# Graph attention and linear attention on one core: all pairs' k projected ahead of all pairs' q

## The chip, the cores and the metric

The kernel runs on one core of a Trainium2 chip. TensorE multiplies matrices, VectorE and ScalarE work on elements, GpSimd (POOL) scatters, and SyncE (SP) issues most of the DMA transfers. Each engine takes its instructions in the order in which they are written, and waits on semaphores that the others raise. The metric is the time of one execution in device microseconds; lower is better.

## The reference, cut to what matters

`x` has 1250 rows of 768. The layer adds to it a graph network (three attention layers over 21250 edges, 4 heads of 192 each), a linear attention of 12 heads of 64 (256 features), and then a mixture of 8 experts. The change touches the linear attention's projections and, beside them, the first steps of the graph attention.

```python
def softmax_kernel(data, proj, is_query):
    data_dash = einsum('bhnd,md->bhnm', d ** -0.25 * data, proj)
    diag = sum(data * data, -1) * 0.5 * (d ** -0.25) ** 2
    m = max(data_dash, -1) if is_query else max(data_dash, (-3, -2, -1))
    return ratio * (exp(data_dash - diag - m) + EPS)
q, k, v = xn @ w_qkv.T                       # 12 heads of 64
q_prime, k_prime = softmax_kernel(q, proj_mat, True), softmax_kernel(k, proj_mat, False)
context, k_sum = einsum(k_prime, v), sum(k_prime)
out = einsum(q_prime, context) / einsum(q_prime, k_sum)
# graph attention, for each layer and head
e = leaky_relu(as_n[src] + ad_n[dst]);  m = segment_max(e, dst);  p = exp(e - m[dst])
out = segment_sum(p / segment_sum(p)[dst] * h[src], dst)
```

For k the greatest product over all rows, features and heads is taken off, so no k feature can be made before the greatest value of all pairs is known. For q it is the row's own greatest.

## The kernel before

**Order.** The whole program is a list of steps, `ORDER`, written by generators (lines 117 to 485). Every engine's program walks the same list and emits its part of each step, so the list fixes the order of each engine's queue. A `None` in a generator ends a tick. `paced(...)` runs tracks side by side, each with a rate: at a rate of 0.5 a track gives one tick's steps in every second tick. `in_step` staggers the stages of one loop by lags. Ticks have no length in time; engines run as fast as their waits allow.

**The projection stage** (`projection_steps`, line 227). Twelve passes n, one for each pair of heads and each of k and q. Before, even n are k and odd n are q of pair n // 2. A pass has three blocks of columns m = 3n + c (512, 512 and 226 rows of `x`), each with two halves of TensorE work (`qk`, 18 products a block). For each block ScalarE squares the result (`sq`) and rounds it (`qk_row`), VectorE splits off the low part (`qk_split`, line 1387), TensorE sums the squares (`norms`, line 993), and VectorE writes `diag`. Once a pass `w_split` splits the weights (`wq_lo`, line 1295). For the greatest value, `k_top` multiplies a finished k by the features, tile by tile (ten tiles a pair), and VectorE reduces each to `kmax` (line 1405). It reads k out of `qk_out`, which SP also stores to DRAM (`qk_store`). At the end `top_max`, `top_turn` and `top_spread` reduce `kmax` over all, transpose, reduce, spread the value over the partitions and write `k_shift`.

**The graph track beside it** (`graph_steps`, line 276). It starts when block `COUNTS_AT` is reached. `tab_in` loads three count tables a tile, `count` adds them on VectorE (three additions, lines 1427 to 1431), ScalarE copies the sum to bf16 (`count16`, line 1871), TensorE transposes it (`count_turn`, line 1028) and VectorE writes `absent` (line 1440). Ten tiles, at `COUNT_RATE`. Then `edge_layer(0)`: 40 edge maxima (`edge_max`, VectorE, line 1452), at `EARLY_EDGE_RATE` while projections run and `FIRST_EDGE_RATE` behind them. `shifts` turns the maxima into shift rows, which go through DRAM and come back by `head_in`.

**Behind the projections** `mix_steps` (line 336) runs at rate 1: for each pair ten k tiles (`dash`, `k_exp`, `k_sum`), ten q tiles (`dash`, `q_exp`, `q_turn`, `q_feat`) and `q_out`/`divide`. Beside it runs `attention_steps` at rate 0.5, which starts only when `shifts(0)` is ordered: items of `edge_z` (VectorE, line 1489), `edge_exp` (ScalarE, line 1882), `weigh` (VectorE, line 1498) and `gather` (TensorE, line 1047, 20 products); after every five items `evict` and `finish` (ScalarE, lines 1896 and 1906). The other layers' edge maxima run at rate 0.6. After the mix come blocks of row products (`row_in`, `row_turn` line 1116, `row_split`, `row_mm`), interleaved with the gathers, since both tracks are in one `paced`.

## Time and profile before

| what | us |
|---|---|
| median of three runs | 1729.6 (1727.94 to 1730.19) |
| the profiled execution | 1718.87 |
| its span | 1717.1 |
| TensorE busy | 1565.3 (91%) |
| VectorE busy | 1129.8 (66%) |
| ScalarE busy | 681.6 (40%) |
| GpSimd busy | 410.1 (24%) |
| TensorE's mean granted clock | 0.973 |

The profile is one execution. Busy time is the time in which an engine ran at least one instruction; matmul ends are modelled. The granted clock is a share of 2.4 GHz: 0.5 is 1.2 GHz, and a value between is a mean over both. In the timeline views the first column is the start, the second the duration (of the whole row, where "x8" stands behind it), and the bracket names the idle time of the engine before it and what ended it. Instructions overlap in their pipelines, so durations do not add up exactly; start-to-start distances do.

### The profile page before, as it was taken

To read this page: it belongs to the slowest core of one execution; us is meant where nothing else is said; L and a number is where in the kernel's file an instruction comes from. 1 tells how busy PE (TensorE), PEld (TensorE's weight loads), DVE (VectorE), ACT (ScalarE), POOL (GpSimd) and SP (SyncE) were. 2 spreads that over 40 slices of the span, in tenths; PEclk is the share of its full clock that TensorE was granted. 3 is DMA by queue.
4 is the path that set the end of the run, shared out by engine and by line. 5 is a ranking of instruction groups with operands and counts; after the bars stand their busy time and mean duration, and the time that the engine had idled before them with its cause. 6 is when DMAs were issued, how large, how long until landed. Compare 5 with 4: busy or idle time off the path is not lost.

```text
span 1717.1 us, 24932 instructions
## 1 busy us (share of the span) xinstructions
PE 1565.3 (91%) x9666; PEld 1192.4 (69%) x9731; DVE 1129.8 (66%) x2573; ACT 681.6 (40%) x1359; POOL 410.1 (24%) x251
## 2 busy tenths in 40 slices
PE   3979999999989789999999979999999999986987
PEld 2556666555655467888888868888888966656664
DVE  6677664114466978797878789767975643885223
ACT  3421001122233467777777754434643431441110
POOL 3788888888400000000000000000000000002331
PEclk9999999999999979999999999999999999996999
DMA  9335545454652223234233044334530133645941
GB/s 353 84 67 118 119 78 118 68 94 65 191 183 87 91 78 135 72 99 131 63 101 95 27 153 134 129 129 151 164 125 29 60 114 135 231 180 211 321 146 50
DMA packets 194504, 213.66 MB, mean 124 GB/s; under 512 B 80975, under 2 KB 149213, under 8 KB 194386
## 3 DMA queue, kind: packets, MB, share of 16 engines
q1 hardware_dynamic: 117762, 187.01, 33.0%
q0 software_dynamic: 75760, 22.70, 8.4%
q10 hardware_dynamic: 864, 2.36, 0.4%
q8 instruction: 77, 1.26, 0.3%
q14 instruction: 41, 0.34, 0.1%
HBM read 144.74 MB, written 68.40 MB: 124 GB/s over the span
## 4 chain that ended last, share of the span: by engine, by line
PE 72%; DVE 17%; ACT 4%; issue 3%; DMA 2%; SPq 1%; POOLq 0%; POOL 0%; ACTq 0%; DVEq 0%
PE bank L1047 19%; PE bank L892 12%; PE bank L893 12%; PE bank L891 12%; PE bank L1217 4%; DVE junk L1452 3%; PE bank L1205 3%; PE bank L1101 3%; PE bank L1073 2%; DVE eb L1498 1%; DVE eb L1489 1%; PE bank L1116 1%; DVE q_max L1521 1%; PE bank L1086 1%; PE bank L993 1%
## 5 line engine op out<-in xcount | busy, mean ns | idle before, releaser
L1047 PE MATMUL bank<-hb,eb 128*128 128x193 f32 (+3 forms) x2400 | 419.9, 332 | 24.7 <-DVE eb L1498 14.0
L1047 PEld LDWEIGHTS bank<-hb,eb 128*128 128x128 f32 (+3 forms) x2400 | 400.3, 190 | 38.3 <-DVE eb L1498 17.1
L2093 POOL DMA_INDIRECT table<-amount,place x170 | 345.1, 2030 | 71.5 <-issue 49.5
L2099 POOL IOTA iota8i<- 128x8 int32 x1 | 0.1, 139 | 934.6 <-DMA node_rows<-node 934.6
L1489 DVE SCALAR_TENSOR_TENSOR eb<-shift_b,as_low,shift_b 128x640 f32<-128x640 f32 (+1 forms) x240 | 196.3, 859 | 7.8 <-DMA shift_b<-shift_rows 7.8
L1882 ACT ACTIVATE eb<-eb,asd 128x640 f32<-128x640 f32 (+1 forms) x240 | 182.0, 814 | 45.9 <-DVE eb L1489 45.9
L1498 DVE SCALAR_TENSOR_TENSOR eb<-eb,count 128x1280 f32<-128x1280 f32 (+1 forms) x120 | 174.4, 1454 | 12.4 <-ACT eb L1882 12.4
L1452 DVE CUSTOM_DVE_ANT_0 junk<-ab,absent 128x1250 bf16<-128x1250 f32 x120 | 174.4, 1453 | 1.0
L891 PE MATMUL bank<-wg_hi,x1T_hi 128*128 128x384 bf16 (+3 forms) x360 | 117.9, 328 | 0.6 <-DVE x1T_lo L1319 0.6
L893 PE MATMUL bank<-wg_hi,x1T_lo 128*128 128x384 bf16 (+3 forms) x360 | 117.9, 327 | 0.0
L892 PE MATMUL bank<-wg_lo,x1T_hi 128*128 128x384 bf16 (+3 forms) x360 | 117.8, 327 | 0.0
L891 PE MATMUL bank<-w_o_hi,aT_hi 128*128 128x384 bf16 (+1 forms) x360 | 117.4, 326 | 0.0
L893 PE MATMUL bank<-w_o_hi,aT_lo 128*128 128x384 bf16 (+1 forms) x360 | 117.3, 326 | 0.0
L892 PE MATMUL bank<-w_o_lo,aT_hi 128*128 128x384 bf16 (+1 forms) x360 | 117.3, 326 | 0.0
L892 PE MATMUL bank<-xnT_lo,wq_hi 128*128 128x512 bf16 (+1 forms) x211 | 72.0, 341 | 3.4 <-DVE wq_lo L1295 2.8
L893 PE MATMUL bank<-xnT_hi,wq_lo 128*128 128x512 bf16 (+1 forms) x215 | 73.4, 341 | 0.3
L1754 DVE TENSOR_TENSOR orow<-bank,b2r 105x384 f32<-105x384 f32 (+1 forms) x32 | 17.8, 556 | 84.5 <-PE bank L1217 76.1
L1333 DVE TENSOR_TENSOR h_row<-bank,bgr 128x384 f32<-128x384 f32 (+1 forms) x60 | 32.5, 555 | 62.1 <-PE bank L893 58.8
L1921 ACT ACTIVATE ef<-bank,q_shift 128x256 f32<-128x256 f32 (+1 forms) x120 | 50.3, 472 | 56.9 <-DVE q_shift L1526 56.9
L891 PE MATMUL bank<-xnT_hi,wq_hi 128*128 128x512 bf16 (+1 forms) x207 | 70.2, 339 | 0.2
L1828 ACT ACTIVATE wg_hi<-stage 128x776 bf16<-128x776 f32 x18 | 15.3, 850 | 132.9 <-DVE stage L1309 118.6
L1921 ACT ACTIVATE ef<-bank,k_shift 128x256 f32<-128x256 f32 (+1 forms) x120 | 49.9, 468 | 37.9 <-PE bank L893 37.6
(288 smaller groups left out, 2944.1 us busy)
## 6 DMA issues: line engine op xcount, KB each, us to landing
w<-in_w SPq DMA_DIRECT2D x16, 1152.0 KB, 20.1
shift_b<-shift_rows SPq DMA_DIRECT2D x24, 625.0 KB, 5.9
h_rows<-h_row SPq DMA_DIRECT2D x27, 388.0 KB
hb<-h_rows SPq DMA_DIRECT2D x12, 873.0 KB
ar<-node_rows SPq DMA_DIRECT2D x27, 384.0 KB
table<-zero POOLq DMA_DIRECT2D x3, 3054.0 KB, 21.1
tab<-table SPq DMA_DIRECT2D x27, 312.5 KB, 3.4
qk_rows<-qk_row SPq DMA_DIRECT2D x12, 625.0 KB
```

Source lines behind the costliest of these rows:

```text
L891: T.matmul(out_ap, lhs[0], rhs[0], start=first, stop=False, skip_group_check=skip)
L892: T.matmul(out_ap, lhs[0], rhs[1], start=False, stop=False, skip_group_check=skip)
L893: return T.matmul(out_ap, lhs[1], rhs[0], start=False, stop=last, skip_group_check=skip)
L1047: ins = T.matmul(bank[w // 2][0:M, c0:c0 + GC + 1], p[0:K, u, w * P:w * P + M], hv[0:K, t, 0:GC + 1], start=opens and u == 0 and w % 2 == ...
L1101: ins = T.matmul(ov[0:R, u, hh, :], qf[q % 4][:, hh * MT + m, 0:R], context[:, m, hh, :], start=u == 0 and hh == 0 and m == 0, stop=m == M ...
L1217: ins = T.matmul(bank[4 + i % 4][0:r1 - r0, 0:HROWS], hT[e % 2][:, f, r0:r1], w2s[e % WEIGHT_SETS][:, f, cs], start=f == 0, stop=f == KF - 1)
L1452: V.tensor_tensor_reduce(out=junk[0:R, :], in0=ab[lh % 2][0:R, :], in1=absent[0:R, t, :], scale=1.0, scalar=-BIG, op0=ALU.add, op1=ALU.max ...
L1489: ins = V.scalar_tensor_tensor(eb[i % EDGE_BUFFERS][:, u, 0:w], low, as_low[:, t, lh:lh + 1], high, ALU.add, ALU.max)
L1498: V.scalar_tensor_tensor(e, e, 1.0, count[:, 2 * pair:2 * pair + 2, ns], ALU.min, ALU.mult).then_inc(sem["edge_w"], 1)
L1882: ins = A.activation(e[:, u, 0:w], e[:, u, 0:w], ACT.Exp, bias=asd[:, t, 8 * l + hh:8 * l + hh + 1])
L1921: ins = A.activation(ef[g % 4][0:R, hh, :], bank[3 + g % 2][0:R, hh * FEATS:(hh + 1) * FEATS], ACT.Exp, bias=bias)
L2093: G.indirect_dma_start(tables[i], bass.IndirectOffsetOnAxis(place[:, c:c + 1], axis=0), amount16[:, c:c + 1], None, compute_op=ALU.add).th ...
```

## The change

The passes are reordered: n = 0 to 5 are k of pairs 0 to 5, n = 6 to 11 are q of pairs 0 to 5. The `k_top` steps of pair n - 1 stand in pass n for n = 1 to 6. k now alternates between both `qk_out` buffers, and the waits on them follow. `top_max`, `top_turn` and `top_spread` move from the end of the projections into pass 7 and 8, `pair_in(0)` (the loads of the first pair's k, v and q) with them. Counts start one block later and run at a rate of 0.6 instead of 0.5, early edge maxima at 0.9 instead of 0.75. `attention_steps` does not wait two ticks behind its first load any more, but until the first pair's tiles (n == 2 NT + 1 in the mix's own order) are through. No instruction is added or taken away.

```diff
--- before.py
+++ after.py
@@ -65,8 +65,8 @@
 SLOT_TILES = 2 * EXPERTS
 NOWHERE = 4096.0
 
-COUNTS_AT = 17
-COUNT_RATE, EARLY_EDGE_RATE, FIRST_EDGE_RATE, EDGE_RATE, ATTENTION_RATE = 0.5, 0.75, 1.1, 0.6, 0.5
+COUNTS_AT = 18
+COUNT_RATE, EARLY_EDGE_RATE, FIRST_EDGE_RATE, EDGE_RATE, ATTENTION_RATE = 0.6, 0.9, 1.1, 0.6, 0.5
 
 
 def rows(t):
@@ -246,9 +246,9 @@
                 yield "qk_split", m - 1
             if part == 0 and c == 0 and n + 1 < 2 * PAIRS:
                 yield "w_split", 30 + n + 1
-            if n % 2 and 2 * c + part:
+            if 1 <= n <= PAIRS and 2 * c + part:
                 for t in range(4 * c + 2 * part - 2, 4 * c + 2 * part):
-                    yield "k_top", NT * (n // 2) + t
+                    yield "k_top", NT * (n - 1) + t
             if part == 0:
                 yield None
 
@@ -259,16 +259,14 @@
     def keep(m):
         if m % NC == NC - 1:
             yield "qk_store", m // NC
-        if m == NC * 4:
+        if m == NC * (PAIRS + 1):
             yield "pair_in", 0
+        for i, name in enumerate(("top_max", "top_turn", "top_spread")):
+            if m == NC * (PAIRS + 1) + i:
+                yield name, 0
 
     yield from in_step([(2, lambda m: [("norms", m)]), (0, product), (1, last_split), (2, keep)],
                        NC * 2 * PAIRS)
-    yield "top_max", 0
-    yield None
-    yield "top_turn", 0
-    yield None
-    yield "top_spread", 0
     done.add("projected")
     yield None
 
@@ -320,8 +318,8 @@
         return []
 
     yield "head_in", 0
-    yield None
-    yield None
+    while "first" not in done:
+        yield None
     yield from in_step([(5, of_half("finish")), (5, mark), (4, of_half("evict")), (0, edge_z),
                         (1, lambda i: [("edge_exp", i)]), (2, lambda i: [("weigh", i)]), (3, lambda i: [("gather", i)])],
                        LH * ITEMS)
@@ -339,6 +337,8 @@
 
     def features(n):
         pair, kind, t = order[n]
+        if n == 2 * NT + 1:
+            done.add("first")
         if kind == "k" and t == 5 and pair + 1 < PAIRS:
             yield "pair_in", pair + 1
         if kind:
@@ -819,7 +819,7 @@
                 k = j - 24
                 return wT_qkv[k * 128:(k + 1) * 128, 2 * D:3 * D]
             n = j - 30
-            c = (1 - n % 2) * D + (n // 2) * 128
+            c = int(n < PAIRS) * D + n % PAIRS * 128
             return wT_qkv[:, c:c + 128].rearrange("(k p) c -> p k c", p=128)
 
         def w_views(j):
@@ -1002,9 +1002,9 @@
             def k_top(i):
                 pair, t = divmod(i, NT)
                 pe.wait_ge("feats_lo", 1)
-                pe.wait_ge("qk_lo", NC * (2 * pair + 1))
+                pe.wait_ge("qk_lo", NC * (pair + 1))
                 pe.wait_ge("k_max", i - 1)
-                dash_into(4 + i % 2, qk_out[0], t).then_inc(sem["top_mm"], 1)
+                dash_into(4 + i % 2, qk_out[pair % 2], t).then_inc(sem["top_mm"], 1)
 
             def top_turn(_):
                 pe.wait_ge("top_v", 1)
@@ -1389,7 +1389,7 @@
 
             def norms(m):
                 n = m // NC
-                which, pair = 1 - n % 2, n // 2
+                which, pair = int(n < PAIRS), n % PAIRS
                 c0, c1 = chunk(m)
                 t0 = c0 // P
                 ve.wait_ge("norm_mm", m + 1)
@@ -1416,7 +1416,7 @@
                 ve.wait_ge("top_pe", 2)
                 V.tensor_copy(top[0:P, 2:3], bank[5][0:P, P:P + 1]).then_inc(sem["top_v"], 1)
                 ve.wait_ge("top_v", 3)
-                ve.wait_ge("diag_in", 2 * PAIRS * NC)
+                ve.wait_ge("diag_in", PAIRS * NC)
                 V.tensor_scalar(k_shift[:, :, :], diag[:, 1, :, :], top[0:P, 2:3], -1.0, ALU.add,
                                 ALU.mult).then_inc(sem["top_v"], 1)
 
@@ -1861,8 +1861,8 @@
                 se.wait_ge("norm_mm", m - 2)
                 A.activation(sq[m % 3][:, 0:c1 - c0], b, ACT.Square).then_inc(sem["qk_square"], 1)
                 se.wait_ge(f"qk_out{n % 2}", 16 * (n // 2))
-                if n % 2 == 0:
-                    se.wait_ge("top_mm", NT * (n // 2))
+                if n >= 2:
+                    se.wait_ge("top_mm", NT * min(n - 1, PAIRS))
                 A.activation(qk_out[n % 2][:, 0, c0:c1], b, ACT.Copy, scale=NORM).then_inc(sem["qk_hi"], 1)
 
             def count_(t):
@@ -2194,7 +2194,7 @@
 
             def qk_store(n):
                 sy.wait_ge("qk_lo", NC * (n + 1))
-                S.dma_start(qk_rows[1 - n % 2, n // 2], qk_out[n % 2][:, :, :]).then_inc(sem[f"qk_out{n % 2}"], 16)
+                S.dma_start(qk_rows[int(n < PAIRS), n % PAIRS], qk_out[n % 2][:, :, :]).then_inc(sem[f"qk_out{n % 2}"], 16)
 
             def tab_in(t):
                 R = rows(t)
@@ -2259,7 +2259,7 @@
                 else:
                     sy.wait_ge("qk_mm", NC * 2 * PAIRS)
                 for j in range(2):
-                    sy.wait_ge(f"qk_out{j}", 16 * (PAIRS if pair else 1))
+                    sy.wait_ge(f"qk_out{j}", 16 * (PAIRS if pair else PAIRS // 2 + 1 - j))
                     sy.wait_ge(f"v_out{j}", 16 * HALF)
                 if pair >= 2:
                     sy.wait_ge("dash_mm", dash_of(pair - 2, "k", NT - 1) + 1)
```

What it does to the order on the engines, at three places on which the prediction rests.

VectorE, while the counts are built: `absent` and `count` are the tables' steps, `qk_row` the split of a block, `kmax` the reduction of a `k_top`. Before, pass 7:

```order
L1387 SCALAR_TENSOR_TENSOR qk_row_194<-bank,qk_row_194 128x512
L1405 TENSOR_REDUCE kmax<-bank 128x1 x4
L1440 TENSOR_SCALAR absent<-bank 128x8x128
L1440 TENSOR_SCALAR absent<-bank 128x128
L1440 TENSOR_SCALAR absent<-bank 98x128
L1427 TENSOR_TENSOR count<-tab_143,tab_144 128x1250
L1429 TENSOR_TENSOR count<-count,tab_230 128x1250
L1431 TENSOR_TENSOR count<-count,ident 128x128
L1397 TENSOR_SCALAR diag<-bank 128x4x2
L1387 SCALAR_TENSOR_TENSOR qk_row_194<-bank,qk_row_194 128x512
L1405 TENSOR_REDUCE kmax<-bank 128x1 x3
```

After, the block of pass 7 that has two counts:

```order
L1387 SCALAR_TENSOR_TENSOR qk_row_194<-bank,qk_row_194 128x512
L1440 TENSOR_SCALAR absent<-bank 128x8x128
L1440 TENSOR_SCALAR absent<-bank 128x128
L1440 TENSOR_SCALAR absent<-bank 98x128
L1427 TENSOR_TENSOR count<-tab_143,tab_144 128x1250
L1429 TENSOR_TENSOR count<-count,tab_230 128x1250
L1431 TENSOR_TENSOR count<-count,ident 128x128
L1409 TENSOR_REDUCE top<-kmax 128x1
L1440 TENSOR_SCALAR absent<-bank 128x8x128
L1440 TENSOR_SCALAR absent<-bank 128x128
L1440 TENSOR_SCALAR absent<-bank 98x128
L1427 TENSOR_TENSOR count<-tab_145,tab_146 128x1250
```

The reductions to `kmax` are gone from between the splits and the counts, and one block now has two count tiles, with `top_max` (line 1409) between.

VectorE, around the end of the first layer's edge maxima (the 98-row maximum of `m_col` is its last; line 1474 is the transpose behind which the shift rows are stored; line 1489 is the first edge step, which needs them back; line 1536 is a `divide` of the mix). Before (the last `divide` stands directly ahead of the first row):

```order
L1452 ISA junk,m_col<-ab_249,absent 98x1250
L1452 ISA m_col 98x1
L1462 TENSOR_TENSOR mz<-m_col,asd 128x40
L1465 SCALAR_TENSOR_TENSOR ms<-mz 128x40
L1469 TENSOR_TENSOR shift<-asd,ms 128x10x4
L1470 SCALAR_TENSOR_TENSOR shift<-asd,ms 128x10x4
L1474 STREAM_TRANSPOSE shift_t<-shift 128x320
L1452 ISA junk,m_col<-ab_248,absent 128x1250
L1452 ISA m_col 128x1
L1452 ISA junk,m_col<-ab_248,absent 128x1250
L1452 ISA m_col 128x1
L1489 SCALAR_TENSOR_TENSOR eb_153<-shift_b_251,as_low,shift_b_250 128x640 x2
```

After:

```order
L1452 ISA junk,m_col<-ab_249,absent 98x1250
L1452 ISA m_col 98x1
L1462 TENSOR_TENSOR mz<-m_col,asd 128x40
L1465 SCALAR_TENSOR_TENSOR ms<-mz 128x40
L1469 TENSOR_TENSOR shift<-asd,ms 128x10x4
L1470 SCALAR_TENSOR_TENSOR shift<-asd,ms 128x10x4
L1474 STREAM_TRANSPOSE shift_t<-shift 128x320
L1536 RECIPROCAL inv<-bank 128x2
L1536 RECIPROCAL inv<-bank 98x2
L1489 SCALAR_TENSOR_TENSOR eb_153<-shift_b_251,as_low,shift_b_250 128x640 x2
L1452 ISA junk,m_col<-ab_248,absent 128x1250
L1452 ISA m_col 128x1
```

The last `divide` moved behind the transpose, and the two edge maxima between the transpose and the first edge step moved behind the edge step.

ScalarE, at the end of the gathers (`eb` is the last items' exponential, `node` lines 1896 and 1906 the last eviction and scaling, `aT_hi` the splits of the first row tiles of the next block). Before:

```order
L1882 ACTIVATE eb_157<-eb_157,asd 128x610 x2
L1970 ACTIVATE w_o_hi<-st_0_242 128x768
L1978 ACTIVATE aT_hi<-bank 128x384 x2
L1896 ACTIVATE node_160<-bank 128x2x193 x2
L1896 ACTIVATE node_160<-bank 98x193
L1970 ACTIVATE w_o_hi<-st_1_243 128x768
L1906 ACTIVATE node_160<-node_160,rinv 128x192 x4
L1906 ACTIVATE node_160<-node_160,rinv 98x192
L1978 ACTIVATE aT_hi<-bank 128x384 x2
```

After:

```order
L1882 ACTIVATE eb_157<-eb_157,asd 128x610 x2
L1896 ACTIVATE node_160<-bank 128x2x193 x2
L1896 ACTIVATE node_160<-bank 98x193
L1906 ACTIVATE node_160<-node_160,rinv 128x192 x4
L1906 ACTIVATE node_160<-node_160,rinv 98x192
L1970 ACTIVATE w_o_hi<-st_0_242 128x768
L1978 ACTIVATE aT_hi<-bank 128x384 x2
L1970 ACTIVATE w_o_hi<-st_1_243 128x768
L1978 ACTIVATE aT_hi<-bank 128x384 x2
```

The first `aT_hi` of the next block moved from ahead of the last eviction to behind the last scaling and a weight copy. On TensorE the transposes of that row tile likewise moved from ahead of the last gather to behind it.

## Rows read from the trace of the kernel before

**Rows 1.** The page, part 1: busy time, share of the span, instructions.

```profile
PE 1565.3 (91%) x9666; PEld 1192.4 (69%) x9731; DVE 1129.8 (66%) x2573; ACT 681.6 (40%) x1359; POOL 410.1 (24%) x251
```

**Rows 2.** Windows: stretch, its length, each engine's busy time, granted clock, DMA.

```profile
461.00:541.00 80.00, 69.29 (x453) 41.94 (x459) 52.05 (x114) 25.35 (x38) 0.00 (x0) 0.96 0.49 158
569.00:577.00 8.00, 2.22 (x13) 1.79 (x15) 7.57 (x15) 0.00 (x0) 0.00 (x0) 0.75 0.48 162
...
620.00:640.00 20.00, 19.17 (x78) 15.17 (x80) 10.71 (x22) 10.48 (x28) 0.00 (x0) 0.52 0.25 69
642.00:665.00 23.00, 19.05 (x111) 13.85 (x112) 20.15 (x30) 17.54 (x35) 0.00 (x0) 0.93 0.75 251
996.00:1055.00 59.00, 45.27 (x236) 42.44 (x236) 57.02 (x78) 30.51 (x56) 0.00 (x0) 0.91 0.47 148
1355.00:1380.00 25.00, 25.00 (x158) 24.74 (x157) 14.20 (x17) 10.71 (x21) 0.00 (x0) 1.00 0.24 83
```

**Rows 3.** VectorE's timeline: the weight splits that open passes 4, 5, 6 and 10.

```profile
431.68 0.95 DVE L1295 TENSOR_TENSOR wq_lo<-stage,wq_hi 128x768 bf16<-128x768 f32 x1
...
443.32 0.96 DVE L1295 TENSOR_TENSOR wq_lo<-stage,wq_hi 128x768 bf16<-128x768 f32 x1
...
461.04 0.95 DVE L1295 TENSOR_TENSOR wq_lo<-stage,wq_hi 128x768 bf16<-128x768 f32 x1
...
540.61 0.95 DVE L1295 TENSOR_TENSOR wq_lo<-stage,wq_hi 128x768 bf16<-128x768 f32 x1
```

**Rows 4.** VectorE's timeline: one block of pass 8, from split to split.

```profile
511.98 0.69 DVE L1387 SCALAR_TENSOR_TENSOR qk_row<-bank,qk_row 128x512 bf16<-128x512 f32 x1 [2.14 <-ACT qk_row L1866]
512.59 0.94 DVE L1440 TENSOR_SCALAR absent<-bank 128x1024 bf16<-128x1024 bf16 x3
...
517.71 0.69 DVE L1387 SCALAR_TENSOR_TENSOR qk_row<-bank,qk_row 128x512 bf16<-128x512 f32 x1 [2.21 <-ACT qk_row L1866]
```

**Rows 5.** ScalarE's timeline in the same block.

```profile
515.46 1.25 ACT L1871 ACTIVATE count<-count 128x1250 bf16<-128x1250 uint16 x1 [3.50 <-DVE count L1431]
516.61 0.58 ACT L1862 ACTIVATE sq<-bank 128x512 f32<-128x512 f32 x1
```

**Rows 6.** TensorE's timeline: last norms behind the tops, and the first feature product.

```profile
568.61 0.95 PE L993 MATMUL bank<-halves,sq 128*128 128x2 f32 x8
...
576.79 0.63 PE L892 MATMUL bank<-feats_lo,k_first 128*128 128x512 bf16 x1 [0.33 <-issue]
```

**Rows 7.** VectorE's timeline: an edge maximum, the shift transpose, the first edge step.

```profile
577.44 1.45 DVE L1452 CUSTOM_DVE_ANT_0 junk<-ab,absent 128x1250 bf16<-128x1250 f32 x1
...
631.57 0.51 DVE L1474 STREAM_TRANSPOSE shift_t<-shift 128x320 f32<-128x320 f32 x1
...
642.78 1.68 DVE L1489 SCALAR_TENSOR_TENSOR eb<-shift_b,as_low,shift_b 128x640 f32<-128x640 f32 x2 [7.84 <-DMA shift_b<-shift_rows]
```

**Rows 8.** ScalarE's timeline: the first output weights' copy.

```profile
1012.04 0.84 ACT L1970 ACTIVATE w_o_hi<-st 128x768 bf16<-128x768 f32 x1 [7.93 <-DMA st<-in_wT_proj]
```

**Rows 9.** VectorE's timeline: its part of the same weights.

```profile
1012.92 0.96 DVE L1541 TENSOR_TENSOR w_o_lo<-st,w_o_hi 128x768 bf16<-128x768 f32 x1 [1.75 <-ACT w_o_hi L1970]
```

**Rows 10.** TensorE's timeline: the last gather and the first row product behind it.

```profile
1375.60 3.45 PE L1047 MATMUL bank<-hb,eb 128*128 128x193 f32 x20
...
1379.55 0.33 PE L891 MATMUL bank<-w_o_hi,aT_hi 128*128 128x384 bf16 x1
```

**Rows 11.** ScalarE's timeline behind the last gather.

```profile
1379.32 0.83 ACT L1970 ACTIVATE w_o_hi<-st 128x768 bf16<-128x768 f32 x1
1381.57 1.84 ACT L1906 ACTIVATE node<-node,rinv 128x192 f32<-128x192 f32 x5 [1.42 <-DVE rinv L1511]
1383.32 0.84 ACT L1978 ACTIVATE aT_hi<-bank 128x384 bf16<-128x384 f32 x2
```

**Rows 12.** VectorE's timeline: the low part of the next row tile.

```profile
1383.82 1.02 DVE L1561 SCALAR_TENSOR_TENSOR aT_lo<-bank,aT_hi 128x384 bf16<-128x384 f32 x2 [2.28 <-ACT aT_hi L1978]
```

**Rows 13.** Who TensorE waited for, whole run: total, times, longest.

```profile
PE bank L891 <- DVE kmax L1405: 4.9, 3, 2.7
```

## Prediction: what the change does to the time

> **What bounds the kernel now.** I read the profile's page first. TensorE is busy for 1565.3 of the 1717.1 us span [rows 1]. Nearly all its work is the same before and after: this change only moves instructions. So the time can change only through TensorE's idle gaps (some 150 us in all) and through stretches at the lower granted clock. I then asked the windows view and the timelines where those are near anything that moves. There are five places. (a) While the counts are built, 461 to 541 us: 69.29 of 80 busy at a granted clock of 0.96, so 10.7 us idle and 3.2 us of clock lost [rows 2]. (b) The last 8 us before the first feature product: 2.22 busy at 0.75 [rows 2]. (c) From there until the edge gathers run: the clock is at 0.52 in 620 to 640, and 4.0 us are idle at 0.93 in 642 to 665 [rows 2]. (d) 996 to 1055 us: TensorE 45.3 of 59, VectorE 57.0 [rows 2]. There VectorE is the bound. (e) 1355 to 1380: TensorE is full [rows 2]. This is where something can be lost.
>
> **Part 1: the top products move (first stage).** Ten `k_top` steps now stand beside each of the passes n = 1 to 6, instead of beside every second pass. The weight split on VectorE occurs once a pass and serves as its stamp. A pass without tops takes 443.32 - 431.68 = 11.64 us, a pass with them 461.04 - 443.32 = 17.72 us [rows 3]. Ten tops are 6.08 us of TensorE work that nothing hides, before and after, so clean passes 1 to 5 only shift: n = 6 starts at 461.0 + 2 x 6.08 = 473.2 us.
>
> Next the counts. Before, n = 6 to 9 took 540.61 - 461.04 = 79.6 us [rows 3]. Clean they would be 2 x 11.64 + 2 x 17.72 = 58.7, and the ten groups of count transposes add some 5.6 (an estimate from how closely their starts follow each other), so about 15 us are lost. The reason is a ring through two in-order engines. VectorE splits a block at 511.98, writes the absence tile at 512.59, adds the counts behind it, and then idles 2.21 us until it splits the next block at 517.71 [rows 4]. It waits because ScalarE copies the count first (515.46, 1.25 us) and only then squares and rounds the next block (516.61) [rows 5]. The ring is 517.71 - 511.98 = 5.73 us for each block that has a count. TensorE's own work there is about 5.0 us for a full block and 2.8 us for a short one. Taking the tops out of the ring does not shorten it.
>
> After, I follow the same ring from 473.2. n = 6 has ten tops and the first two counts, about 25.6 us (12.1 clean until the first count, then 13.5 for two rings with the last four tops in them). n = 7 takes 6.5 (with the weight split), 5.7, and 10.2 for a block with two counts, where the second absence tile waits for a copy and a transpose (1.25 + 0.7): 22.4. n = 8 takes three rings, a weight split and the other `top_` steps (0.7), 18.6. n = 9 has one ring and is clean behind it, 10.3. That is 76.9 us, so pass 10 starts at 550.1. `pair_in(0)` now goes out on SP among the tables' loads: four transfers, some 1.9 MB by the buffers' sizes. The DMA engines are at 0.49 there [rows 2] and each table has a whole ring to land, so I cost it at nothing; a table that came late would lengthen the ring by as much (in the bound below). Passes 10 and 11 carry edge maxima but no tops. VectorE needs 6 x 1.51 + 3.1 (splits, norms, weights) = 12.2 us against TensorE's 11.64, so I take 2 x 11.64: products done at 573.4, of which the norms are the last 0.95, so 572.5. Before, they ended at 568.6 [rows 6]. The passes themselves are 3.9 us later.
>
> **Part 2: the greatest value goes out of the gap.** Before, TensorE's norms began at 568.61 and the first product with `k_first` at 576.79 [rows 6], 8.2 us later. The transpose, the spread and their three VectorE steps, each with an edge maximum between, were in it. What is late next is the last block's norm values: `dash` waits for all of `diag_in`, and on VectorE two splits and three edge maxima of 1.51 us each [rows 7] stand ahead of them. Counted back that is 4.9 us after the products' end, so 577.4. Parts 1 and 2 together: +0.6 us. Bounds: -3 (the ring runs 0.3 us shorter with fewer VectorE steps in it) to +3 (the two idle stretches of 4.3 us that I find in blocks 23 and 26 also cost clock).
>
> **Part 3: edges against mix, first gathers.** The edge track now has two more edge maxima ordered ahead, but VectorE has not done them at 577.4. It has one less to do before the transposes (the order above shows both places) and one more ahead of the first `q_exp`, so the mix's q stage is 1.7 us later. The transposes also no longer stand behind the last `divide`, and end at about 629.2 instead of 632.0. The transfers from there to the first edge step take 642.78 - 631.57 = 11.2 us [rows 7], so it starts at 640.0. It now stands directly behind the transposes. `edge_exp(0)` is behind it on ScalarE with `k_exp(1,4)` queued behind that, and TensorE's `dash(1,k,6)` waits for it. Price: 3 us idle and about 2 us more at the low clock. The mix is two tiles (3.5 us of TensorE) less far when the edge steps start, 2.8 us earlier: +0.7. The gain: gathers begin near 651 instead of 660, so the 4.0 us idle and about 2.3 us of clock in [rows 2]'s 642 to 665 go. Sum to 665: +0.7 - 6.3 + 5 = -0.6 us; this includes the +0.6. Bounds: -4 (no stall behind the edge step) to +4 (nothing regained).
>
> **Part 4: the VectorE-bound stretch.** One edge maximum fewer (1.5 us) falls in it. Also ScalarE waited 7.93 us for the output weights [rows 8], because `head_in(6)` went out on SP just before them; now `head_in(6)` is ordered before the last `att` store. VectorE idled only 1.75 us of that [rows 9]. I take -2.5 us, between 0 and -3.3.
>
> **Part 5: the end of the gathers.** The gathers end six steps earlier against the rows. Before, `row_turn(20)` stood ahead of the last gather on TensorE, and its splits on ScalarE ahead of the last scaling. The gather began at 1375.60 and the row product followed at 1379.55 [rows 10]. After, ScalarE does the last eviction, the five scalings and a weight copy before it reaches `aT_hi`. From the gather's end (1379.05): the last eviction is over when the weight copy starts at 1379.32, the reciprocals take 0.5 (estimate), the scalings 1.84, the weight copy 0.83, `aT_hi` 0.84 [rows 11] and `aT_lo` 1.02 [rows 12], the last two in part side by side. Row product at about +5.5, less the 0.65 of the transpose: 5 us idle. Nothing else is ready for TensorE, and the rows behind it fill it fully. Add 1.5 us at the low clock: 569 to 577 at 0.75 gives 8 x 0.25 = 2.0 us as the most that a gap of this size showed [rows 2]. Total +6.5, bounds +4 to +9.
>
> Another row speaks for more: 620 to 640 stayed at 0.52 though TensorE was busy for 19.17 of 20 us [rows 2]. If the row products stayed low as long, part 5 would be 5 + 20 x 0.48 = 14.6 us. I take it for unlikely, since the projections, which are dense like the row products, had full clock again within a few us after each gap. The Trainium skill, "TensorE: Matmul & The Clock Gate", Part 1, says that the throttled state is the default and that activity releases it. By that rule part 5 keeps the 1.5 us; the trace agrees behind the projections' gaps and disagrees in 620 to 640.
>
> **The sum.** -0.6 - 2.5 + 6.5 = +3.4 us. Against the profiled execution's own 1718.87 us (span 1717.1) this is 1722.3. That execution is 10.7 us under the median of the three runs. I add the difference, not a ratio: 1729.6 + 3.4 = 1733.0 us.
>
> **Rivals.** *The earlier gathers win.* If the count ring shortens to TensorE's own work where the tops are gone (three full blocks at 0.7 us, -2), part 3 gives its lower bound (-4) and part 4 -3, against +4 in part 5, the sum is -5: 1724.6. For it speaks the 8.2 us gap, the plainest hole in the trace. Against it: the ring is held by ScalarE's order, which the change leaves. *The tail decides, slower.* The price is the empty TensorE behind gather 119, up to 9 us, with part 3 giving nothing (+2) and part 4 -2: +9, so 1738.6. It decides as soon as parts 1 to 4 give back less than about 3 us. *The moves cancel.* The clean passes and the rows are TensorE-bound, the tail gap is only its idle 4 to 5 us with no clock lost, and the front gives as much back: 0, so 1729.6. This is also what comes out if the tops in the ring had been the real cause of part (a)'s waits (4.9 us behind `kmax` in the whole run [rows 13]) and their going pays for the tail.
>
> **How the numbers follow.** Forecast 0.45 (half of it below and half above the bound of 3.5 us), tail 0.2, cancel 0.17, gathers win 0.18. A measurement of this kernel can tell about 0.2%, 3.5 us, from no change. Faster: 0.18. Same: 0.17 + 0.22 = 0.39. Slower: 0.23 + 0.2 = 0.43. The range leaves out the outer halves of both side cases: 1724 to 1739.
>
> **What would show it.** Right: a ring of about 5.7 us a block while the counts run, with two TensorE gaps of about 4 us; the first `k_first` product within 2 us of 577; first gather near 651; 5 us of idle TensorE between the last gather and the next row product, ended by `aT_lo`. Wrong: passes 7 and 8 at 12 to 15 us each, a row product that follows the last gather at once, or a wait on the tables' transfers because `pair_in(0)` now goes out among them.

## The result: slower, and where the time went

| | before | after |
|---|---|---|
| median of five runs, us | 1727.94 (1723.72 to 1730.19) | 1740.76 (1733.67 to 1741.61) |
| ratio | | 1.0086, 95% interval 1.0061 to 1.0112 |
| profiled execution | 1718.87 | 1741.61 |

The forecast was 1733.0 with a range up to 1739; the direction was the likeliest of the three and the size was too small. The two profiled executions lie 22.7 us apart, the medians only 12.8. So the shown profile of before can't be laid beside the one of after without care. I therefore profiled the unchanged kernel again (`b_again`, 1726.16 us, close to its median). Below, "second profile" means that one. One slow run, of `b_late_rows` (1782.79 us), is left out of its row of the table below.

The page of the changed kernel, its span and its part 1:

```profile
span 1739.8 us, 24931 instructions
...
PE 1582.3 (91%) x9664; PEld 1205.5 (69%) x9731; DVE 1130.2 (65%) x2573; ACT 680.3 (39%) x1359; POOL 410.5 (24%) x251
...
PEclk9989999999999778999999999999999999996999
```

TensorE has 17 us more busy time than in [rows 1] for the same instructions. That is the clock: the same products last longer at half clock (a row product lasts 0.53 us behind the gap in the rows below, and 0.33 us in the second profile). The last line is the granted clock in tenths over 40 slices; the 7, 7, 8 lie at 565 to 696 us.

I cut both programs at the same events and laid the stretches side by side. The changed kernel (stretch, length, busy time of PE, PEld, DVE, ACT, POOL, granted clock, DMA share, GB/s):

```profile
476.91:556.09 79.18, 63.40 (x425) 40.61 (x430) 47.53 (x110) 25.46 (x38) 0.00 (x0) 0.94 0.57 187
556.09:581.96 25.87, 22.69 (x148) 14.96 (x149) 22.60 (x42) 5.56 (x12) 0.00 (x0) 1.00 0.23 90
581.96:608.10 26.14, 23.89 (x103) 17.29 (x103) 20.16 (x28) 16.56 (x31) 0.00 (x0) 0.61 0.33 108
608.10:662.48 54.38, 46.50 (x234) 34.73 (x239) 41.29 (x75) 35.04 (x82) 0.00 (x0) 0.73 0.44 145
662.48:1007.50 345.02, 327.90 (x2173) 298.29 (x2205) 282.21 (x434) 249.93 (x548) 0.00 (x0) 1.00 0.25 78
1007.50:1069.54 62.04, 50.94 (x295) 48.72 (x295) 59.52 (x82) 33.55 (x64) 0.00 (x0) 0.92 0.46 145
1069.54:1388.58 319.04, 315.68 (x1963) 270.59 (x1962) 227.07 (x305) 137.54 (x250) 0.00 (x0) 0.99 0.34 115
1388.58:1397.83 9.25, 1.97 (x13) 1.70 (x11) 3.78 (x13) 4.78 (x11) 0.96 (x6) 0.82 0.49 140
```

The second profile of the kernel before, from the same events to the same events:

```profile
462.50:543.99 81.49, 70.80 (x458) 42.30 (x456) 51.63 (x114) 25.36 (x38) 0.00 (x0) 0.94 0.45 147
543.99:579.76 35.77, 30.33 (x184) 18.61 (x182) 27.88 (x53) 5.56 (x12) 0.00 (x0) 0.96 0.18 67
579.76:606.48 26.72, 24.70 (x106) 17.48 (x105) 20.11 (x30) 16.56 (x31) 0.00 (x0) 0.60 0.33 104
606.48:668.28 61.80, 51.41 (x293) 36.95 (x294) 49.20 (x90) 41.83 (x98) 0.00 (x0) 0.84 0.42 136
668.28:989.72 321.44, 311.36 (x2091) 281.98 (x2089) 266.53 (x410) 237.95 (x518) 0.00 (x0) 1.00 0.25 81
989.72:1056.18 66.46, 51.16 (x296) 48.81 (x295) 60.33 (x80) 33.84 (x66) 0.00 (x0) 0.92 0.34 112
1056.18:1386.84 330.66, 326.16 (x2030) 280.94 (x2028) 239.10 (x323) 146.06 (x264) 0.00 (x0) 0.99 0.37 119
1386.84:1387.34 0.50, 0.50 (x7) 0.49 (x5) 0.00 (x0) 0.46 (x2) 0.00 (x0) 1.00 0.24 92
```

The events are: weight split of pass 6, of pass 10, first `k_first` product, first `q_max`, first gather, last `q_max`, first `row_turn`, end of the last gather, next row product. The two programs are 1.5 us apart ahead of anything that changed, which is taken off below. Four readings. (1) From the first `k_first` product to the end of the gathers the two need 806.6 and 807.1 us: the change moves work between these stretches and saves nothing. (2) All passes with the gap behind them cost +0.7 us (12.9 more ahead of pass 6, 2.3 and 9.9 less behind it). (3) The stretch behind the first feature product runs at a clock of 0.6 in both; the shown profile of before had 0.92 there, and that is where most of its head start comes from. (4) The last stretch is 9.25 us against 0.50. It is the one place where the change plainly loses. Behind it the changed kernel needs 4.9 us more up to its end: 1.7 at a low clock in the first row products, and 3.3 in the row products of the last tiles, where its clock fell and that of the second profile didn't (last section). With these the stretches add up to the 15.4 us between the two spans (1739.8 and 1724.4).

The tail itself, the changed kernel's TensorE, ScalarE and VectorE behind the last gather:

```profile
1388.42 0.82 PE L1116 MATMUL bank<-ident,ar 128*128 128x128 f32 x6
1396.52 1.51 PE L1116 MATMUL bank<-ident,ar 128*128 128x128 f32 x6 [7.28 <-DVE aT_lo L1561]
1397.83 0.53 PE L891 MATMUL bank<-w_o_hi,aT_hi 128*128 128x384 bf16 x1
```

```profile
1388.62 0.33 ACT L1896 ACTIVATE node<-bank 98x193 f32<-98x193 f32 x1 [0.17 <-PE bank L1047]
1389.51 1.83 ACT L1906 ACTIVATE node<-node,rinv 128x192 f32<-128x192 f32 x5 [0.55 <-DVE rinv L1511]
1391.25 0.83 ACT L1970 ACTIVATE w_o_hi<-st 128x768 bf16<-128x768 f32 x1
1391.98 0.84 ACT L1978 ACTIVATE aT_hi<-bank 128x384 bf16<-128x384 f32 x2
```

```profile
1392.11 0.96 DVE L1541 TENSOR_TENSOR w_o_lo<-st,w_o_hi 128x768 bf16<-128x768 f32 x1 [2.63 <-ACT w_o_hi L1970]
1395.33 0.19 DVE L1584 MEMSET stats<- 128x160 f32 x1 [2.27 <-POOL iota_i L2102]
...
1395.84 1.01 DVE L1561 SCALAR_TENSOR_TENSOR aT_lo<-bank,aT_hi 128x384 bf16<-128x384 f32 x2
```

ScalarE does what the prediction wrote down: last eviction, scalings, weight copy, `aT_hi`. But VectorE doesn't follow at once. It stands 2.27 us in the set-up of the expert stage (`expert_setup`), which waits for GpSimd's iota, and spends 0.5 us on it, with `aT_lo` queued behind. GpSimd in its turn waits there, for the store of the last head's rows, which can go out only behind the scalings:

```profile
1394.75 0.14 POOL L2099 IOTA iota8i<- 128x8 int32 x1 [942.74 <-DMA node_rows<-node]
```

The set-up ends the attention track. Before, VectorE came to it behind the low part of this row tile and of the next one, and now it comes to it ahead of both.

### The profile page after: what moved, and what is told of

It is laid out like the page before. It is cut to its first block, busy times and chain, and to the rows that moved or that the text cites. A ratio compares the mean times of both kernels' runs of the same rounds, so it can differ in the third digit from the quotient of the medians.

```text
span 1739.8 us, 24931 instructions
## 1 busy us (share of the span) xinstructions
PE 1582.3 (91%) x9664; PEld 1205.5 (69%) x9731; DVE 1130.2 (65%) x2573; ACT 680.3 (39%) x1359; POOL 410.5 (24%) x251
## 4 chain that ended last, share of the span: by engine, by line
PE 71%; DVE 17%; ACT 5%; issue 3%; DMA 3%; SPq 0%; POOL 0%; POOLq 0%; ACTq 0%; DVEq 0%
PE bank L1047 17%; PE bank L892 13%; PE bank L893 13%; PE bank L891 12%; PE bank L1217 4%; PE bank L1205 3%; DVE junk L1452 3%; PE bank L1073 2%; PE bank L1101 2%; DVE eb L1489 2%; DVE eb L1498 2%; PE bank L1116 1%; DVE q_max L1521 1%; ACT ef L1921 1%; PE bank L993 1%
## 5 line engine op out<-in xcount | busy, mean ns | idle before, releaser
L1047 PEld LDWEIGHTS bank<-hb,eb 128*128 128x128 f32 (+3 forms) x2400 | 399.9, 190 | 36.0 <-DVE eb L1498 15.4
L1333 DVE TENSOR_TENSOR h_row<-bank,bgr 128x384 f32<-128x384 f32 (+1 forms) x60 | 32.4, 555 | 64.8 <-PE bank L893 64.8
L1405 DVE TENSOR_REDUCE kmax<-bank 128x1 f32<-128x512 f32 (+1 forms) x60 | 40.1, 691 | 47.7 <-PE bank L893 47.7
## 6 DMA issues: line engine op xcount, KB each, us to landing
w<-in_w SPq DMA_DIRECT2D x16, 1152.0 KB, 12.2
```

The lines of the kernel that those rows point to most:

```text
L1047: ins = T.matmul(bank[w // 2][0:M, c0:c0 + GC + 1], p[0:K, u, w * P:w * P + M], hv[0:K, t, 0:GC + 1], start=opens and u == 0 and w % 2 == ...
```

## The experiments

Fifteen variants ran, and the unchanged kernel once more for its profile (`b_again`). All ratios are to runs of the kernel before on the same chip. The two last columns come from each run's span and mean granted clock: "clock lost" is span x (1 - clock), "rest" is the remainder, both means over the runs (the kernel before: 59.1 and 1666.7 over 119 runs). They tell whether a kernel loses by the clock or by work and waits; idle time at half clock counts half in each.

| kernel | median us | ratio (95% interval) | clock lost | rest |
|---|---|---|---|---|
| changed | 1740.76 | 1.0086 (1.0061 to 1.0112) | 65.0 | 1672.4 |
| `b_start` | 1742.5 | 1.0083 (1.0055 to 1.011) | 67.3 | 1672.1 |
| `b_rates` | 1732.8 | 1.0028 (1.0009 to 1.0047) | 64.0 | 1666.4 |
| `b_passes` | 1726.35 | 1.0002 (0.9985 to 1.0019) | 58.7 | 1666.5 |
| `a_ticks` | 1730.16 | 1.0025 (1.0008 to 1.0042) | 57.5 | 1670.9 |
| `b_late_rows` | 1737.96 | 1.0058 (1.0037 to 1.0079) | 64.8 | 1671.5 |
| `b_start_tail` | 1734.1 | 1.0027 (1.0013 to 1.0041) | 64.5 | 1667.1 |
| `a_tail` | 1732.09 | 1.002 (1.0007 to 1.0034) | 62.4 | 1667.0 |
| `a_setup` | 1738.72 | 1.0058 (1.0038 to 1.0077) | 65.1 | 1671.3 |
| `a_late_evict` | 1733.41 | 1.0035 (1.0019 to 1.0052) | 63.5 | 1668.0 |
| `a_hold` | 1728.27 | 1.002 (0.9997 to 1.0042) | 60.8 | 1667.5 |
| `b_fill` | 1724.54 | 0.9982 (0.9968 to 0.9996) | 51.5 | 1671.3 |
| `a_tail_fill` | 1726.65 | 0.9981 (0.9968 to 0.9995) | 52.4 | 1671.5 |
| `p_fill` | 1727.33 | 0.9994 (0.9977 to 1.0011) | 56.4 | 1668.8 |
| `b_fill2` | 1729.34 | 1.001 (0.9994 to 1.0025) | 35.7 | 1692.0 |
| `p_fill2` | 1731.31 | 1.0023 (1.0003 to 1.0043) | 42.2 | 1687.6 |

**The parts of the change, one at a time.** Names with `b_` start from the kernel before, with `a_` from the changed one.

`b_start` takes only the start of the attention:

```diff
+        if n == 2 * NT + 1:
+            done.add("first")
...
     yield "head_in", 0
-    yield None
-    yield None
+    while "first" not in done:
+        yield None
```

> The kernel before with one part of the change alone: the attention track starts when the first pair's tiles are through instead of two ticks behind its load. Passes, top products and rates are as before. It takes four ticks out, so the last gathers are ordered 4 ticks ahead of the rows' next tile instead of beside it. Theory A (the tail: with the gathers ahead, ScalarE does the last eviction and the scalings before it rounds the next row tile, and TensorE has nothing): a gap of 4 to 9 us between the last gather and the next row product, and a time 3 to 8 us above the kernel before. Theory B (the front: the loss comes from TensorE idling and running at the low granted clock between 500 and 665 us, and the start of the attention is a side matter): within 2 us of the kernel before, or faster by up to 3.

`a_ticks` is the reverse, the changed kernel with the two `yield None`.

> The changed kernel with the attention start undone (two ticks behind the load again), everything else as changed. Theory A (tail): the gap behind the last gather shrinks from 9.25 us to under 3, since the next row tile's rounding is ordered ahead of the last scalings again, and the time falls 5 to 9 us below the changed kernel, to some 1733. Theory B (front): the gap may shrink, but the low clock from 582 to 602 us and from 637 to 662 us stays, and the time stays within 4 us of the changed kernel's 1740.8.

`b_passes` has the passes, tops and greatest value moved, with the old start and the old rates; `b_rates` has only the line of rates and `COUNTS_AT`.

> The kernel before with the passes alone reordered (all k first, then all q, tops beside n = 1 to 6, the greatest value in passes 7 and 8); rates, start of the counts and start of the attention as before. Theory A (tail): no gap behind the last gather, since that order is as before; 1728 plus or minus 2. Theory B (front): shorter idle ahead of the first feature product, but the granted clock is at 0.5 for some 20 us behind it, and the count ring loses as much as in the changed kernel; 5 to 10 us above the kernel before.

> The kernel before with the rates alone changed: counts a block later at 0.6, early edge maxima at 0.9. The passes keep their order, so each second pass has both tops and counts. It also moves the attention four ticks ahead against the rows. Theory A (tail): a gap of 3 to 8 us behind the last gather, and 2 to 7 us slower. Theory B (front): denser counts lengthen the stretch of the counts by at most 2 us and the clock stays as in the kernel before, so within 3 us of it.

Measured: one small part, the start of the attention, makes as large a loss alone (1.0083, 14.9 us, more than either theory had). The condition itself never waits, since the pair's tiles are ordered through before it is asked; what it does is to leave out two empty ticks of a track at half rate, four ticks of the list. Undoing it in the changed kernel brings 1730.16, below what I had expected of either theory. The reordering of the passes, the bulk of the change, makes no difference (1.0002). The gaps behind the last gather fell in step with how far the gathers had moved ahead of the rows: 0 ticks none, 2 ticks (`a_ticks`) 0.94 us idle, 4 ticks (`b_start`, `b_rates`) 4.81 us, 6 ticks (changed) 7.28 us. The 5.2 us that `b_rates` loses are of the size of its gap, though they stand in the clock's column and not in the rest; I can't say what paid for the idle time there. `b_start` has the same gap and loses 14.9 us, three times as much, so theory A isn't the whole of it. The parts don't add up to the change (14.9 + 5.2 - 1.3 = 18.8 us against 12.8 measured). Start and rates each move the gathers four ticks ahead and make 4.81 us of idle time, and both together 7.28 us and not 9.62; that is 2.3 us of the 6.0, and the rest stays open.

**The tail by itself.** `b_late_rows` moves nothing but the third block of row products:

```diff
+        if l == 1:
+            for _ in range(6):
+                yield None
         yield from row_block(l + 1)
```

> The kernel before with six empty ticks of the mix track ahead of the third block of row products; nothing else moved, so the last gathers end six ticks ahead of the rows. It prices the tail by itself. Theory A: a gap of 5 to 9 us between the last gather and the row product and a time 6 to 9 us above the kernel before. Theory C (TensorE has as much idle elsewhere to make good): a gap, but under 2 us slower.

`a_tail` and `b_start_tail` hold the last gathers back instead (3 ticks of the track in the one, 2 in the other):

```diff
+        if i == 112:
+            for _ in range(3):
+                yield None
         yield "edge_z", i
```

> The changed kernel with the attention track held for three of its own ticks ahead of item 112, so the last gathers stand beside the rows' next tile again (as in the kernel before) and everything up to there is as changed. Theory A (the tail is what the change loses): the row product follows the last gather within 1 us, and the time falls by 7 to 10 us against the changed kernel, to some 1732. Theory B (the tail is a part, the clock behind the first products and the edges the rest): it falls by 3 to 6 us. Theory C (the gap only takes the place of idle elsewhere, as behind the late rows' products): it falls by less than 2.

> The kernel before with the early start of the attention, and the attention held for two of its own ticks ahead of item 112, so that the last gathers stand against the rows as in the kernel before. With the start alone it was 1.0083 of the kernel before (1742.5 us). Theory A (tail): the gap of 6.7 us goes and with it half or more of the loss: 1732 to 1736. Theory B (the early start itself, by the clock and by ScalarE's queue among the first pairs' tiles): 1738 or more.

Measured: +9.3 us for the tail alone, with the same 7.28 us of idle TensorE; 8.7 us back in the changed kernel and 8.4 in `b_start_tail`. The row product followed the last gather after 0.50 us again in both. In all three the "rest" moved by about 5 us (4.8, 5.4, 5.0). That is theory A for the tail, and theory C (a gap that costs nothing) is out. Left over are 3.4 us in `a_tail` and 5.4 in `b_start_tail`.

**What the gap is made of.** `a_setup` puts four empty ticks of the track ahead of `expert_setup`; `a_late_evict` puts four ahead of the last `evict`, so that only the last eviction, the scalings and the set-up move behind the row tile, and all gathers stay.

> The changed kernel with the set-up of the expert stage ordered 8 ticks later, behind the next row tile's rounding instead of ahead of it. In the trace of the changed kernel VectorE waits 2.27 us for GpSimd in that set-up and spends 0.5 us on it, with the low part of the row tile behind it. If that wait is a term of the tail: the idle time behind the last gather falls from 7.3 to 4.5 to 5 us and the time by 2 to 4 us, to some 1737. Rival (ScalarE's scalings alone set the end, the set-up is hidden): 7 us stay and the time is the same.

> The changed kernel with only the last eviction and the last scalings (and the set-up behind them) ordered 8 ticks later; all gathers and edge steps stay where they are. If the order on ScalarE and VectorE alone makes the tail: a gap of 2 us or less behind the last gather and 7 to 10 us less, 1731 to 1734, as when the gathers were held back. Rival (the gap is there because TensorE has done its gathers too early, whatever the others do): 4 us or more of idle stay, and less than 4 us are gained.

TensorE's idle row behind the last gather in `a_setup`, then in `a_late_evict` (all with a shifted line number for the same `row_turn`):

```profile
1394.20 1.22 PE L1118 MATMUL bank<-ident,ar 128*128 128x128 f32 x6 [4.44 <-DVE aT_lo L1563]
```

```profile
1391.07 0.92 PE L1119 MATMUL bank<-ident,ar 128*128 128x128 f32 x6 [0.94 <-DVE aT_lo L1564]
```

The idle time went from 7.28 to 4.44 to 0.94 us, and the median from 1740.76 to 1738.72 to 1733.41. So the order on ScalarE and VectorE alone makes the tail, and the set-up with its wait for GpSimd is 2.8 us of its idle time. The 2.0 us of `a_setup` in the median has overlapping intervals; its gap is shown, its gain in time only likely. `a_late_evict` is left 5.6 us above the kernel before on its chip, `a_tail` 3.4, with overlapping intervals.

**The rest.** `a_hold` holds the attention at its start instead of its end (three more ticks behind the `while`), so that it stands against mix and rows as before, with all else changed.

> The changed kernel with the attention held for three more of its own ticks at its start, so that it stands against mix and rows as in the kernel before; passes, greatest value and rates stay changed. If the rest of 3 to 5 us comes from the early start: within 2 us of the kernel before (1726 to 1730), waits of the gathers for evictions of about 6 us instead of 8 between the first gather and the last greatest value of a q row, and no gap at the end. Rival (it comes from the reordered front and its counts): 1731 to 1733.

Measured: 1728.27, a median at the kernel before's (1727.83). The ratio, 1.002 with an interval of 0.9997 to 1.0042, is that of `a_tail`, and the mean span is 2.8 us over that of the kernel before on the same chip, so the time alone doesn't show that the early start carries the rest. The profiles do better. From the shift transpose to the first gather, the changed kernel and then `a_hold`:

```profile
636.97:662.48 25.51, 23.81 (x91) 17.78 (x92) 14.31 (x21) 16.11 (x32) 0.00 (x0) 0.50 0.86 283
```

```profile
637.84:668.17 30.33, 24.94 (x146) 16.50 (x146) 22.39 (x35) 23.79 (x49) 0.00 (x0) 0.89 0.78 257
```

All five profiles with the changed front and the early start are at 0.50 or 0.61 there (`a_setup`, `a_late_evict`, `a_tail` and `a_tail_fill` are the others), and the two with the same front and the attention held back are at 0.92 (`a_ticks`) and 0.89. Length times (1 - clock) is 9 to 13 us in the one group and 2 to 3 in the other (the work between the two events isn't quite the same, since the attention stands elsewhere against the mix). Part of that is lost again elsewhere: over the whole run the changed kernel has 65.0 us of clock lost, `a_ticks` 57.5 and `a_hold` 60.8. Up to 3 us for the reordered passes (the upper end of `b_passes`, 1.0019) isn't excluded.

The waits are seen best with the tail out of the way. Who TensorE waited for between the first gather and the last `q_max`, in the second profile and then in `b_start_tail` (its lines are five further down):

```profile
PE bank L1047 <- ACT node L1896: 5.8, 7, 1.2
PE bank L1086 <- ACT ef L1921: 3.6, 4, 1.6
```

```profile
PE bank L1052 <- ACT node L1901: 9.2, 8, 2.0
PE bank L1091 <- ACT ef L1926: 5.8, 7, 1.5
```

In both rows TensorE waits for ScalarE: for the eviction of a finished head, and for the exponentials of a q tile. With the attention four ticks ahead, the evictions meet the mix's steps in ScalarE's queue otherwise, and 5.6 us more are lost; 4 us come back later, where VectorE bounds. In the changed kernel the same rows read 8.0 and 6.2. `a_hold` came as expected here. Between its own first gather and last `q_max` (668.17 to 990.60):

```profile
PE bank L1049 <- ACT node L1898: 5.8, 7, 1.2
PE bank L1088 <- ACT ef L1923: 3.4, 3, 1.6
```

So with the front as changed the waits go back when the attention does, though I can't name one pair of steps that makes them (`b_passes`, with the old start, has 7.7 and 2.5). What they cost in time is another question. Of the 5.4 us left in `b_start_tail` only 0.6 stand in the rest and 4.1 in the clock lost (64.5 and 667.1 against 60.4 and 1666.5 for the kernel before on that chip). The waits nearly all come back, and what remains goes by the clock; why it falls lower with the early start is open.

**The clock behind the first products.**

> The kernel before, unchanged, for a second look at its profile. The shown profile of it took 1718.87 us, below nearly all its timed runs. Theory B (its clock behind the first feature products was unusual): the stretch from the first feature product to the first greatest value of a q row takes some 26.5 us with 10 us lost to the clock, not 20.2 with 1.6, as in the kernels that keep its order up to there, and the time is about 1728. Theory E (the shown profile is typical and the low clock came with the edits): 20 us again, and about 1719.

It came as theory B said: 26.72 us at 0.60 (above), not 20.18 at 0.92, and 1726.16 us. The next kernel, `b_fill`, asks for the cause. It adds unread products ahead of the waits, on TensorE alone:

```diff
+            def fill(count):
+                pe.wait_ge("absent_in", 2 * NT)
+                for _ in range(count):
+                    T.matmul(bank[6][:, :], xnT[0][:, 0, 0:P], feats[0][:, :], start=True, stop=True)
```

> The kernel before with 31 extra products of 512 columns (0.22 us each at full clock), whose results nobody reads, put into TensorE's idle time between the last projection and the first sum over k features: 8 ahead of the last norms, 8 and 6 ahead of the steps of the greatest value, 2 ahead of the first feature product, 7 ahead of the first sum. They add work but should fill idle time only. Theory B (a low clock of some 20 us behind that gap, set off by the idle, costs 7 to 10 us in most executions): the granted clock stays at 1.0 from the projections' end to 600 us, and the time falls 5 to 9 us, to some 1720. Theory D (the low clock there comes whatever TensorE did before): the clock falls all the same and the time is the same or up to 3 us more.

The stretch behind the first feature product in the shown profile of before:

```profile
576.79:596.97 20.18, 17.55 (x111) 11.81 (x112) 19.62 (x29) 16.35 (x31) 0.00 (x0) 0.92 0.40 131
```

`b_fill`, the 36 us ahead of the first feature product and the stretch behind it:

```profile
545.63:581.64 36.01, 35.01 (x205) 20.37 (x207) 28.13 (x53) 5.56 (x12) 0.00 (x0) 1.00 0.18 68
581.64:601.98 20.34, 18.59 (x121) 12.65 (x122) 19.78 (x29) 16.36 (x31) 0.00 (x0) 1.00 0.42 134
```

With TensorE busy for 35.0 instead of 30.3 us, the clock never falls, and the stretch takes 20.34 instead of 26.72 us. Against the runs of the kernel before on the same chip (60.4 and 1666.5) the clock lost falls by 8.9 us, the rest grows by 4.8 (idle time at half clock counts half in it, and the fill adds some), and the median falls by 4.1 us. Theory D is out: it is the idle time ahead that sets the low clock. The Trainium skill, "TensorE: Matmul & The Clock Gate", Part 1, has it that the throttled state is the default and activity releases it; these rows agree in that the clock is at 0.60 behind the gap and at 1.00 behind the filled one. That activity alone releases it they don't bear out: TensorE was busy for 24.70 of the 26.72 us at 0.60.

The same fill in `a_tail`, in `b_passes` (`p_fill`), and a second fill of 112 products of 128 columns in the last stage (`b_fill2`, `p_fill2`):

> The changed kernel with the last gathers held back (as in the run before: 1732.1 us, 1.0020) and 22 extra products of 512 columns in TensorE's idle time between the last projection and the first sum over k features. Theory A+B (the tail and the low clock behind the first products are separate losses and add up): the clock stays at 1.0 up to the first q tile, and the time falls by another 3 to 6 us, to 1726 to 1729; against the kernel before with the same fill (1724.5) what is left of the change costs 2 to 4 us. Theory F (the reordered front gains once both are out of the way): 1722 or less.

> The reordered passes alone (1726.35 us, 1.0002), with 17 extra products of 512 columns in the idle time between the last projection and the first sum over k features. If the fill is worth here what it was in the kernel before: the clock stays at 1.0 up to the first q tile, and 3 to 6 us less, 1720 to 1723, the best of all. Rival (the run with both fills, 1731.3 against 1729.3 for the kernel before, shows that the passes lose elsewhere once the clock is kept): 1725 to 1727.

> The kernel before with the fill ahead of the first feature products (1724.5 us) and 112 more extra products of 128 columns in float32 in the idle time of the last stage, around the last tile's ranking and the map of slots, where the clock is at 0.5 for some 17 us of 35. Theory B (idle sets the low clock, wherever it is): the clock stays at 1.0 through the last stage, and the time falls by another 4 to 9 us. Theory D: no change of the clock there, and the same time or up to 3 us more.

> The reordered passes alone (1726.35 us, 1.0002) with both fills. Theory B: as the kernel before with both fills, within 2 us, since the passes alone changed nothing. Theory F (the shorter gap ahead of the first feature product pays once its clock is kept): 3 us or more below the kernel before with both fills.

`a_tail_fill` came as expected, 5.4 us under `a_tail`: tail and clock are separate losses. By ratio it equals `b_fill` (0.9981 and 0.9982), so with tail and gap both out of the way 0 to 2 us are left of the change. `p_fill2` came within 2.0 us of `b_fill2`, as theory B had it.

`b_fill2` itself missed. The last stage from the last full tile's routing products to the first expert products, and from there to the end, first without (`b_fill`) and then with the second fill:

```profile
1542.65:1574.16 31.51, 14.38 (x146) 12.96 (x145) 24.88 (x76) 4.31 (x12) 6.83 (x6) 0.59 0.28 86
1574.16:1719.30 145.14, 125.08 (x564) 91.05 (x564) 42.68 (x65) 17.16 (x39) 40.82 (x42) 0.96 0.63 196
```

```profile
1544.20:1584.53 40.33, 36.94 (x369) 36.12 (x369) 27.72 (x78) 4.20 (x12) 6.79 (x6) 0.92 0.35 124
1584.53:1725.80 141.27, 121.16 (x566) 86.88 (x564) 39.99 (x62) 17.19 (x39) 40.93 (x42) 0.98 0.59 186
```

The clock rises from 0.59 to 0.92 as theory B has it, and the stretch behind is 3.9 us shorter, but the filled stretch itself is 8.8 us longer. TensorE is busy for 36.94 us of it against 14.38: the fill adds 22.6 us of work where 17.1 us were idle. The transposes of the last row tile, which had waited 3.81 us for VectorE, now start 7.59 us behind the first event and not 5.22. A smaller fill there wasn't tried. `p_fill` missed too, and came nearer to its rival: the clock held up to the first q tile and then 7.8 us were lost in the q stage (0.79 there), against 3.5 in `b_passes` (0.90), so more than half of the 6.9 us that `b_passes` loses behind the first product (0.71 over 23.81 us) was lost again in the next 37 us. I have no cause for that.

The fastest kernel is the kernel before with the first fill, 1724.54 us, 0.9982 (0.9968 to 0.9996): a gain that is just above what can be told from none, and it comes from no part of the change. `a_tail_fill` has the same ratio.

## Why the prediction was too low, point by point

In the prediction's own terms, parts 1 to 4 were to give back 3.1 us and part 5 to cost 6.5. By time everything but the tail costs 3.4 us (`a_tail`), and the tail 8.7. The step that failed is the gain of parts 3 and 4, -1.2 and -2.5 us behind the first feature product, of which 0.5 came. There the runs show more clock lost ahead of the first gather and more idle time behind it; part 5 was too small by another 2.2 us, for a set-up step that I left out.

**The passes: right.** Pass 6 began 12.9 us later (12.2 worked out), passes 6 to 9 took 79.2 us (76.9), with the ring at 5.72 us a block (splits at 508.20 and 513.92). Passes and gap together cost +0.7 us against the second profile, +0.6 in the text. `b_passes` confirms it by time.

**Parts 2 and 3: the start was right, the rest was not.** The first `k_first` product came at 581.96, 0.7 us later than in the second profile once the start's 1.5 is off. But the step "first gather near 651" failed. VectorE's first edge step and TensorE's first gather in the changed kernel:

```profile
648.88 1.68 DVE L1489 SCALAR_TENSOR_TENSOR eb<-shift_b,as_low,shift_b 128x640 f32<-128x640 f32 x2 [9.55 <-DMA shift_b<-shift_rows]
```

```profile
662.48 4.20 PE L1047 MATMUL bank<-hb,eb 128*128 128x193 f32 x20
```

The first edge step follows the transposes (636.97) by 11.9 us, 11.2 in the text. What was wrong is when both began: the low clock behind the first products, 3 us long in the profile that I worked on, lies ahead of them. Against the second profile, with the start's 1.5 us off, the transposes are 5.6 us earlier (2.8 in the text) and the first gather 7.3 us earlier (9 in the text), so the order did what I said. Its price was wrong. Length times (1 - clock) of the two stretches from the first feature product to the first gather is 24.9 us in the changed kernel and 20.6 in the second profile, 4.3 more; the text had the low clock at 620 to 640 alone, with 2 us more and 2.3 us less after the change. In the changed kernel's profile the clock stays at 0.50 for the whole 25.5 us from the transposes to the first gather, and with the attention held back it is at about 0.9. And the gain that I booked for the gathers' earlier start, 6.3 us, doesn't exist in the sum: from the first feature product to the end of the gathers, 0.5 us is gained.

**Part 4: seen, and given away.** ScalarE's wait of 7.93 us for the output weights [rows 8] is gone (7.78 in the second profile):

```profile
1033.40 0.83 ACT L1970 ACTIVATE w_o_hi<-st 128x768 bf16<-128x768 f32 x1
```

The stretch around it is 4.4 us shorter, but the one ahead of it, from the first gather, has 7.0 us more idle TensorE (17.12 against 10.08; 5.3 if `a_setup`, with the same order up to there and more matmul records in its trace, is taken instead). I had booked the first and not looked for the second: the early start makes the gathers wait more for ScalarE's evictions. `b_start_tail`, the early start with the tail taken out, costs 5.4 us in all, most of it in the clock lost. The early start's own price is the second term that was missing.

**Part 5: right mechanism, size too small.** 5 us of idle and 1.5 of clock were forecast; 7.28 and 1.67 came. The missing part is `expert_setup`: I followed ScalarE's queue to its end, and VectorE's only for `aT_lo`. Without the set-up the idle time is 4.44 us. Behind the gap 1.7 us more went at low clock among the row products. By time the tail is worth 8.7 us: the rival "the tail decides" (+9, 1738.6) was the right case, and the point that I gave for it (the front gives back less than 3 us) was met. It had 0.2 and deserved more: two of my three gains rested on one execution's idle rows.

**The base: nearly right by luck.** I added the difference to the median, not to the profiled time. But the profile it was worked out on had a clock behind the first products that the second profile and the others with that order didn't have; the 10.7 us between profile and median should have made me ask where a usual execution spends them. They were in the place that part 3 priced. The base was also 1.7 us above the median of five (1727.94), which hid part of the miss: the time was off by 7.8 us and the difference by 9.4.

## What to carry to other kernels

When a track is moved by a few steps against another, follow every in-order queue at the far end of the program too, down to steps that have nothing to do with either (here a set-up that waited for GpSimd, and GpSimd for a store). A change of two empty ticks outweighed the reordering of twelve passes; measure such riders apart from the main edit. And when a profiled execution is well below the median, find out which stretch was lucky before pricing anything in it.

## What the runs showed of the hardware

The same instructions behind the same idle gap were once at full clock and otherwise at half. In the shown profile the clock fell during the 8 us gap [rows 6] and was back 3 us behind the first feature product:

```profile
577.00:580.00 3.00, 2.13 (x5) 0.45 (x3) 2.93 (x7) 2.06 (x3) 0.00 (x0) 0.53 0.95 319
580.00:596.97 16.97, 15.21 (x106) 11.20 (x108) 16.48 (x23) 14.29 (x29) 0.00 (x0) 1.00 0.29 96
```

In five other profiles with that order it stayed low through some 20 us in which TensorE was over 90% busy (0.60 over 26.7 us, above). In the seven profiles with reordered passes and no fill the same stretch came out at 0.61 to 0.77. Only filling the gap kept the clock up in every profile taken (five of five).

The last row tile shows the same on a smaller scale. Its transposes and the row products behind them, after an idle wait of 1.28 us in the changed kernel and of 1.36 us in the second profile:

```profile
1544.02:1552.75 8.73, 8.73 (x58) 5.53 (x58) 6.20 (x23) 4.80 (x10) 0.00 (x0) 0.80 0.36 128
```

```profile
1530.15:1537.20 7.05, 7.05 (x57) 4.94 (x58) 6.03 (x23) 4.80 (x10) 0.00 (x0) 1.00 0.45 158
```

The executions of the kernel before spread from 1718 to 1734 us (119 runs), and their spans fall as their mean clock rises: about 1717 us at 0.973, 1725 to 1729 at 0.965. Which stretches make that up no run shows beyond the two profiles.
